# A gated delta-rule layer with a feed-forward block on one core: weights kept on chip for the eight items of a head, values turned on VectorE by way of DRAM, keys scaled on GpSimd, and all stages and transfers in a new order

## The reference

```python
qkvz = hidden_states @ W_qkvz          # per key head: q 128, k 128, v 2 x 128, z 2 x 128
mixed = silu(conv4(concat(q, k, v)))   # causal convolution over 4 tokens
beta, g = sigmoid(b), -exp(A_log) * softplus(a + dt_bias)
q, k = l2norm(q) * DK ** -0.5, l2norm(k)     # each key head serves two value heads
# by chunks of 64 tokens (the kernel takes chunks of 128):
T = inverse(I + tril(k_beta @ k.T * decay, -1))
v_new, k_cumdecay = T @ v_beta, T @ (k_beta * exp(g))
# step over the chunks of a sequence:
vn = v_i - k_cumdecay_i @ state
out = (q_i * exp(g_i)) @ state + (q_i @ k_i.T * decay_i) @ vn
state = state * exp(g_last) + (k_i * exp(g_last - g_i)).T @ vn
x = rmsnorm(core * silu(z)) * norm_weight
y = x.reshape(B, S, VD) @ W_out
```

## Time and profile before

| what | value |
|---|---|
| median of 3 runs | 4410.59 us (4410.58 to 4412.84) |
| time of the profiled execution | 4409.74 us |
| its span, first to last instruction | 4408.0 us |
| TensorE busy, weight loads | 4208.9 us (95%), 3698.7 us (84%) |
| ScalarE busy | 3843.0 us (87%) |
| VectorE busy | 3727.2 us (85%) |
| GpSimd busy | 2342.4 us (53%) |
| moved by DMA | 584.82 MB, mean 133 GB/s |

### The profile page before, as it was taken

How to read it: one execution, slowest core, us unless ns; L and a number is a source line. 1 busy time by engine, 2 the same in 40 slices (tenths; PEclk the granted TensorE clock), 3 DMA queues, 4 the chain that set the end, 5 groups by cost and what they waited for, 6 DMA issues and landing times. The chain is left out here.

```text
span 4408.0 us, 140088 instructions
## 1 busy us (share of the span) xinstructions
PE 4208.9 (95%) x44246; PEld 3698.7 (84%) x44246; DVE 3727.2 (85%) x6642; ACT 3843.0 (87%) x10855; POOL 2342.4 (53%) x3319
## 2 busy tenths in 40 slices
PE   3799999999999999999999999999999999999888
PEld 2688888888888888888888888888888888888745
DVE  5688888888888888888888888888888888888766
ACT  2699999999999999999999999999999999999755
POOL 3355555555555555555555555555555555555455
PEclk9999999999999999999999999999999999999999
DMA  5544444444444444444444434344444343434201
GB/s 182 180 131 146 130 145 133 142 134 141 134 140 135 140 135 140 139 136 139 136 142 132 145 130 146 129 143 132 147 128 150 125 153 122 153 123 154 72 6 34
DMA packets 450786, 584.82 MB, mean 133 GB/s; under 512 B 237472, under 2 KB 315552, under 8 KB 433184
## 3 DMA queue, kind: packets, MB, share of 16 engines
q1 hardware_dynamic: 449568, 575.59, 40.6%
q10 hardware_dynamic: 1152, 8.39, 0.5%
HBM read 533.81 MB, written 50.07 MB: 132 GB/s over the span
## 5 line engine op out<-in xcount | busy, mean ns | idle before, releaser
L1014 DVE SCALAR_TENSOR_TENSOR conv<-ps,cws,conv 128x511 f32<-128x511 f32 (+2 forms) x1536 | 1085.6, 742 | 59.8 <-ACT conv L892 39.9
L698 PE MATMUL ps<-xb,wb 128*128 128x512 f32 x3072 | 842.9, 409 | 25.7 <-DMA wb<-w_scratch 21.6
L698 PEld LDWEIGHTS ps<-xb,wb 128*128 128x128 f32 x3072 | 542.0, 190 | 127.5 <-issue 27.8
L1057 DVE CAST_PREDICATED pl<-masks,ps 128x512 f16<-128x512 uint16 x768 | 546.9, 712 | 55.3 <-PE ps L760 32.7
L953 ACT ACTIVATE t<-ps 128x512 f16<-128x512 f32 x768 | 465.9, 607 | 118.3 <-PE ps L768 107.1
L1263 POOL TENSOR_TENSOR xo<-xo,zs 128x512 f32<-128x512 f32 x128 | 163.8, 1280 | 717.0 <-DVE xo L1108 717.0
L1263 POOL TENSOR_TENSOR xo<-xo,home 128x512 f32<-128x512 f32 x128 | 162.8, 1272 | 699.4 <-DVE xo L1108 699.4
L957 ACT ACTIVATE u<-ps 128x512 f16<-128x512 f32 x768 | 473.2, 616 | 43.6 <-PE ps L773 43.6
L858 PE MATMUL ps<-wo,xt 128*128 128x256 f32 x3072 | 427.4, 289 | 33.6 <-DVE xt L1114 32.8
L712 PE MATMUL ps<-wb,xb 128*128 128x256 f32 x3072 | 428.5, 289 | 0.0
L858 PEld LDWEIGHTS ps<-wo,xt 128*128 128x128 f32 x3072 | 382.9, 190 | 47.7 <-issue 42.0
(11 more groups left out here) (188 smaller groups left out, 11701.8 us busy)
## 6 DMA issues: line engine op xcount, KB each, us to landing
xb<-x_scratch SPq DMA_DIRECT2D x128, 1024.0 KB, 5.9
wb<-w_scratch SPq DMA_DIRECT2D x128, 1024.0 KB, 5.6
decays<-rows_scratch SPq DMA_DIRECT2D x128, 512.0 KB, 3.7
wb<-w_scratch SPq DMA_DIRECT2D x128, 512.0 KB, 4.3
wo<-wout_scratch SPq DMA_DIRECT2D x128, 512.0 KB, 6.3
rk<-rk_scratch SPq DMA_DIRECT2D x128, 256.0 KB, 4.2
w_scratch<-wsplit SPq DMA_DIRECT2D x128, 192.0 KB, 3.2
wpiece<-in_Wqkvz SPq DMA_DIRECT2D x128, 96.0 KB, 2.5
```

The source lines that it names most:

```text
L698: last = nc.tensor.matmul(proj_bank[c][:, :], wb[:, pw, k * WCOL + c * D:k * WCOL + (c + 1) * D], xb[p][:, px, k * S:(k + 1) * S], start=( ...
L1014: nc.vector.scalar_tensor_tensor(out=conv[c][:, back:S], in0=proj_bank[c][:, 0:S - back], scalar=cws[p][:, c * TAPS + 3 - back:c * TAPS + ...
L1057: nc.vector.copy_predicated(halves(pl[l], l, 0), mask[:, None, :, :].broadcast_to([128, NU, C // (4 << l), 2 << l]), packed(p_bank, l)).th ...
```

## The change

1. Weights are loaded once per head: `load_w`, `load_wz` and `load_wout` do nothing for seven items of eight. `wo` is one buffer instead of two. SP runs a loop of eight steps (`steps_by_head`) for it.
2. The values are no longer turned on TensorE. `flip_v` on VectorE transposes 32x32 blocks of each `conv[V0]`, `conv[V1]` into `flip` (the memory of `et`), `store_v` writes the 512 KB to DRAM, and `load_v` reads them back in four transfers so that each token's channels come together in `vt[p]`, now laid out by 32-channel pieces. `values` on ScalarE is gone. `decay` now waits until the previous item's `store_v` has landed, since both use `et`.
3. `keys` runs on GpSimd.
4. `ORDER` is new in all its parts, offsets now from -3 to 2 (before from -2 to 3); PSUM banks are dealt anew, and the waits that guard them with it. `load_x` now stands at offset +1 in the first part of a step.

```diff
-        wo = [sb(f"wo{p}", [128, 2, R, H], f32r) for p in range(2)]
+        wo = sb("wo", [128, 2, R, H], f32r)
-        vt = [home[:, 1, :].rearrange("p (n h d) -> p n h d", n=NC, h=R), sb("vt1", [128, NC, R, D])]
+        vt = [home[:, 1, :].rearrange("p (w x) -> p w x", w=4), sb("vt1", [128, 4, R * NC * 32])]
+        flip = et[:, :, :].rearrange("p (q u) c -> p q (u c)", q=4)
-        proj_bank = (ps[5], ps[6], ps[5], ps[6])
-        z_bank = (ps[5], ps[6])
+        proj_bank = (ps[6], ps[7], ps[5], ps[7])
+        z_bank = (ps[6], ps[6])
-        turn_bank = (ps[7], ps[5], ps[7], ps[5])
-        gram_bank = (ps[6], ps[7])
-        o_turn_bank = (ps[7], ps[7])
-        out_bank = (ps[7], ps[7])
+        turn_bank = (ps[6], ps[7], None, None)
+        gram_bank = (ps[6], ps[5])
+        o_turn_bank = (ps[7], ps[5])
+        out_bank = (ps[5], ps[7])
...
-            + at(0, ("fix_mm", g1), ("ff_total", 0), ("fix", g0)) + at(1, ("project_z", g1)) + at(2, ("load_wz", 0)) + at(3, ("load_x", 0))
+            + at(-1, ("load_v", 0), ("ff_load", 2), ("ff_load", 0), ("fix_mm", g0), ("residual", 0)) + at(1, ("load_x", 0)) + at(-2, ("gate", g1))
...
-            def load_w(a, p, _):
+            def load_w(a, q, _):
+                if q:
+                    return
+                ws_out.wait(sp, a + B - 1 - LEAD, 32)
                 proj_mm.wait(sp, a - 1, 4)
-                rk_in.wait(sp, a - 1, 16)
...
+            def store_v(a, p, _):
+
+                sp.wait_ge(flipped.sem, flipped.at(a, 2))
+                vt_in.wait(sp, a - 1, 64)
+                sp.dma_start(v_dram[:, :, :], flip).then_inc(v_out.sem, 16)
+
+            def load_v(a, q, _):
+                p = q % 2
+                sp.wait_ge(v_out.sem, v_out.at(a, 16))
+                res_ready.wait(sp, a - 2, NC)
+                for w in range(4):
+                    sp.dma_start(vt[p][:, w, :], v_dram[w * 32:(w + 1) * 32].rearrange("r q x -> q r x")).then_inc(vt_in.sem, 16)
...
-            def values(a, p, h):
-                act.wait_ge(turn_mm.sem, turn_mm.at(a, h + 3))
-                res_ready.wait(act, a - 2, NC)
-                nc.scalar.activation(vt[p][:, :, h, :], four(turn_bank[V0 + h]), ACT.Copy).then_inc(vt_ready.sem, 1)
-
             def decay(a, p, g):
                 act.wait_ge(row_masked.sem, row_masked.at(a, g + 1))
                 act.wait_ge(cw_ready.sem, cw_ready.at(a, 1))
                 attn_ready.wait(act, a - 1, g + 1)
+                v_out.wait(act, a - 1, 16)
...
-            def keys(a, p, _):
-                ve.wait_ge(rk_in.sem, rk_in.at(a, 16))
+            def flip_v(a, p, h):
+
+                ve.wait_ge(silued.sem, silued.at(a, h + 3))
+                attn_ready.wait(ve, a, 2)
+                nc.vector.transpose(flip.rearrange("p q (h n c) -> p h q n c", h=R, n=NC)[:, h],
+                                    conv[V0 + h][:, :].rearrange("p (n q c) -> p q n c", n=NC, q=4)).then_inc(flipped.sem, 1)
...
                 if n == 0:
-                    ve.wait_ge(vt_ready.sem, vt_ready.at(b, 2))
+                    ve.wait_ge(vt_in.sem, vt_in.at(b, 64))
...
+            def keys(a, p, _):
+                pool.wait_ge(rk_in.sem, rk_in.at(a, 16))
+                pool.wait_ge(silued.sem, silued.at(a, 1))
+                ks_mm.wait(pool, a - 2, 3)
+                nc.gpsimd.tensor_tensor(kq[p][:, :, 0, :], conv[K][:, :].rearrange("p (n c) -> p n c", n=NC),
+                                        rk[:, :].rearrange("p (c n) -> p n c", n=NC), ALU.mult).then_inc(kq_ready.sem, 1)
```

More of the change, by code:

```diff
@@ L573, in delta_rule @@
-            + at(1, ("conv", V1, 3)) + at(0, ("u_copy", 5)) + at(1, ("mask_row", g1), ("keys", 0)) + at(0, ("t_copy", 5), ("ff_abs", 0),
-               ("ff_abs", 1)) + at(-1, ("intra_mm", 3)) + at(0, ("resid_mm", g0)) + at(1, ("turn", Q)) + at(-1, ("added", g0), ("out", 3),
-               ("ff_below", 2), ("ff_tern", 2)) + at(0, ("ff_set", 0), ("resid_mm", g1)) + at(1, ("gram", g0)) + at(-1, ("gate", g1))
-            + at(1, ("gram", g1)) + at(0, ("resid", g0)) + at(1, ("decay", g0), ("squares", Q), ("decay", g1)) + at(2, ("load_rows", 0))
@@ L581, in delta_rule @@
-            + at(2, ("project", K)) + at(0, ("y_copy", 0)) + at(1, ("u_first", g0)) + at(0, ("update_mm", 0), ("intra_mm", 0))
+            at(-1, ("t_mm", 5), ("u_mm", 5), ("z", g1)) + at(0, ("conv", V0, 3)) + at(-1, ("rnorm", Q)) + at(-2, ("o_rnorm", g0))
+            + at(-1, ("t_copy", 5), ("ff_abs", 0), ("ff_abs", 1), ("u_copy", 5)) + at(-3, ("out_mm", g0)) + at(-1, ("resid_mm", g0))
+            + at(0, ("conv", V1, 3)) + at(-1, ("resid_mm", g1)) + at(-2, ("intra_mm", 3)) + at(0, ("turn", Q), ("decay", g0), ("gram", g0))
@@ new lines, in delta_rule @@
+            + at(1, ("load_w", 0)) + at(-3, ("added", g0)) + at(0, ("squares", Q)) + at(-2, ("o_norm", g0)) + at(-1, ("resid", g0), ("resid", g1))
+            + at(-2, ("out", 3), ("ff_below", 2), ("ff_tern", 2)) + at(-1, ("ff_set", 0)) + at(0, ("gram", g1), ("system", g0), ("attn", g0))
+            + at(-1, ("load_v", 0), ("ff_load", 2), ("ff_load", 0), ("fix_mm", g0), ("residual", 0)) + at(1, ("load_x", 0)) + at(-2, ("gate", g1))
+            + at(0, ("decay", g1), ("system", g1)) + at(-1, ("fix_mm", g1), ("ff_total", 0)) + at(0, ("diagonal", g0)) + at(-1, ("fix", g0))
@@ L582, in delta_rule @@
+            + at(-1, ("out", 2)) + at(0, ("t_mm", 4)) + at(-1, ("residual", 3), ("ff_tern", 1), ("o_square", g0)) + at(0, ("t_copy", 4), ("u_mm", 4))
+            + at(1, ("conv", V0, 2)) + at(-1, ("qs_mm", 3), ("y", 3)) + at(0, ("p_mm", 5), ("z", g0), ("u_copy", 4)) + at(-1, ("q_part", 3))
+            + at(0, ("store_v", 0)) + at(1, ("conv", V1, 2), ("load_norm", 0), ("silu", Q)) + at(0, ("p", 5)) + at(-1, ("y_copy", 3))
+            + at(1, ("keys", 0)) + at(0, ("project_z", g1))
         )
@@ L598, in steps, with steps_by_head, step @@
                 step(s, s % 2)
+        def steps_by_head(engine, **parts):
+            def step(s, q):
+                for offset, stage, *n in ORDER:
+                    if stage in parts and not (isinstance(s, int) and not 0 <= s + offset < ITS):
+                        parts[stage](s + offset, (q + offset) % B, *n)
+            first, last = -(-(3 - NEAR) // B), (ITS - FAR) // B
+            for s in range(-FAR, first * B):
+                step(s, s % B)
+            with engine.Fori(first, last) as j:
+                for q in range(B):
+                    step(B * j + q, q)
+            for s in range(last * B, ITS - NEAR):
+                step(s, s % B)
         @block.sync
@@ L1179, in ff_ternary @@
                     link(nc.vector.tensor_tensor(m["fs"][:, 1:2], fscale[:, 0:1], fsud[:, :], ALU.mult))
[L1180 removed]
+            steps(ve, ff_set=ff_set, ff_halves=ff_halves, ff_below=ff_below, ff_tern=ff_ternary, conv=convolve, flip=flip_v, system=system, attn=attention, u_first=first, t_first_copy=t_first_copy, p=factor,
                   resid=resid, fix=fix, residual=residual, state=state, out=output, x_low=x_low, added=add)
```

136 lines of the change are left out of this document (69 added, 67 removed).

## The result

The changed kernel takes 4835.99 us (median of 4 runs, 4823.1 to 4841.23) against 4411.72 us (4410.58 to 4413.55) for the one before: ratio 1.0957, interval 1.0944 to 1.097. It is 424 us slower, and 524 us over the forecast. The profiled execution took 4823.1 us.

What follows compares the result with a forecast made beforehand. TensorE's own list of work was taken to set the period (30.99 of 31.42 us per step). Sum: 4410.6 - 116 (turns) + 10 (head starts) + 8 (start) = 4312 us; 8-in-10 range 4240 to 4450, forecast's own 4255 to 4385.

Steps and rivals of the forecast that it cites:

- The input, `load_x`: Input load between `project_z` g1 and the keys' projection: 7.45 us of room, 5.9 to 6.1 needed; cost 0.
- The late rival: Input or values land late on SP's queue; TensorE waits 1.5 us per step for `xb`: 4504 us, chance 0.20.
- Turns off TensorE, 0.91 us per item: Removing the two turns of values shortens TensorE's list by 0.91 us per item: 116 us less.
- packs tighter: Rival: TensorE's idle time goes to zero (floor 30.08 us per step), head starts cost nothing: 4247 us, chance 0.09.
- The order, "I let it stand": New `ORDER`: TensorE's 0.43 us of idle time per step may grow or go; left unchanged in the sum.
- VectorE as the bound: Rival: flips of 2.1 us each make VectorE set a period of 32.2 us: 4530 us, chance 0.06.
- Keys on GpSimd at 1.15: `keys` on GpSimd takes 1.15 us (between 1.04 and 1.28), hidden before `gram` with 2 to 3 us left.
- Values by DRAM: Store and reload of values take 9.3 us after the second flip; `residual` 0 waits 0 to 1.4 us; cost 0.
- Weights once per head, 0: Dropping 7/8 of 2 MB of weights per item gains 0, since no steady-stretch step waited for them.
- Head starts, 10 us more: At a head's first item, `wb` delays `load_v` and `load_x`; about 0.6 us reaches TensorE at 16 heads: 10 us more.
- `u_first`: No-change rival: `u_first` in its long form holds TensorE's `t_first`, giving back 0.82 us per step: 4417 us, chance 0.07.
- Start, 8 us: At program start, `yacc` loads of 8.59 us stand ahead of the third item's input: 8 us more.

Runs made afterwards that it cites:

- experiment 9: Changed kernel with the four `load_v` transfers cut by 32 tokens instead of 32 channels, so each begins with a dimension of 32: 4333.31 us, ratio 0.9824.
- experiment 5: Changed kernel with four `load_v` transfers in 1 KB pieces, the 128 rows first (values land in wrong places): 4288.53 us, ratio 0.9715.
- (3): Changed kernel with `load_v` as one plain 512 KB transfer, rearrangement left out (values land in wrong places): 4227.17 us, ratio 0.9582.
- experiment 6: Changed kernel with the rearrangement moved into the store (four transfers of 32 partitions) and one plain `load_v`; complete layer: 4240.04 us, ratio 0.9608.
- experiment 4: Changed kernel with eight extra 128x512 matmuls on TensorE just ahead of its wait for the input `xb`: 4685.65 us, ratio 1.0621.
- experiment 11: Kernel before, in its old order, with only the values' way exchanged for flips, the rearranging store and one plain load: 4471.39 us, ratio 1.0124.
- experiment 8: Kernel before with only `keys` moved to GpSimd, at its old place in the order: 4464.97 us, ratio 1.0114.
- experiment 1: Changed kernel with the input loaded for the first two items only, so later items use the wrong sequence: 4326.92 us, ratio 0.9808.
- experiment 2: Changed kernel with `load_x` issued ahead of `load_v` in SP's order: 5172.08 us, ratio 1.1724.
- experiment 7: Kernel before with only `wb` loaded once per head (both transfers), order as before: 4424.86 us, ratio 1.0024.
- experiment 10: Experiment 6 with `wb` loaded for each item again (both transfers), `wo` still once per head: 4291.68 us, ratio 0.9718.

## Why the prediction was wrong

**The step that failed** is in "*The input, `load_x`*": "The transfer needs 5.9, or 6.1 with the wake. If SP is free, 1.3 us remain." The room was as worked out (7.2 us from issue to need). The 5.9 us were not: they came from transfers with no narrow one just ahead, and the values' load keeps a quarter of the DMA engines busy for 6 us. The step of 2011.25 of the changed kernel shows it, with the four `load_v` issued from 1999.59 and the input at 2002.11:

```profile
2001.50:2004.00 2.50, 2.50 (x37) 2.32 (x36) 0.90 (x3) 2.35 (x5) 2.29 (x4) 1.00 0.27 95
2004.50:2007.00 2.50, 2.50 (x20) 2.32 (x18) 2.12 (x5) 2.49 (x14) 1.84 (x3) 1.00 1.07 315
2008.00:2009.00 1.00, 1.00 (x10) 1.00 (x10) 0.33 (x2) 1.00 (x8) 0.16 (x1) 1.00 0.27 109
```

Counted by size in the same trace, the packets in flight at a time are at first about four of 1 KB (values), then twelve of 8 KB (input) beside the four, and from 2008 to 2010 four of 8 KB: the last quarter of the input stood in line behind the values. In experiment 9 sixteen of 8 KB are in flight at once. The input took 9.2 us, and the experiments tie this to the first dimension of the values' load: with all rows first it is 6.6 (experiment 5), by 32 rows 6.4 (9), plain 5.6 (3). The prediction counted `load_v` as four issues of SP and 3.5 us to land, never as a load on engines that another transfer needs.

The Trainium skill (DMA: Bandwidth & Descriptors, "Why a DMA increments its semaphore by 16 and not by 1") has the rule that the prediction lacked: the number of DMA engines of a transfer is the largest one up to 16 that divides the slowest dimension on both sides. For the source `q r x` with a 4 in front, and 128 rows in the target, that is 4 of 16; the share of 0.25 to 0.27 and the four packets in flight agree, and so does the 0.75 with 32 in front. The page adds that such a transfer takes the lowest-numbered engines, by which all four parts would share the same four; the share fits, but no run here shows which engines they were.

**What the wait cost** had two parts, one of which the prediction did not have at all. TensorE's idle time is 3.0 us per step, 2.57 more than forecast. The slower clock behind it makes its list 31.53 us long, 1.45 more than the forecast floor and 1.69 more than the 29.84 of the same list in experiment 6; experiment 4 gives back at least 1.2 of it.

**The late rival** ("the input or the values come late", 0.20) had the place and the sign, and 4504 us. Its reason was wrong: it had the store taking 6.3 us, and the store took the 3.7 of the forecast. Its size was half of the wait (1.5 of 3.0 us) and nothing for the clock. That it named the right place is luck as far as its reason goes.

**The rest of the sum**, judged by experiment 6, where the input is in time:

- *Turns off TensorE, 0.91 us per item*, counted in full: "packs tighter", with 4247 us and a chance of 0.09, is what experiment 6 came to (4240.04), partly by luck. Its floor of 30.08 us was too high; TensorE is busy for 29.84 of 29.89 us, 24 us less in 128 steps than 30.08, and the rest of the program takes 17 us more than that case had. Where the 0.24 us come from was not tried.
- *The order, "I let it stand"*: this was a term, not a rest. The turns taken out of the old order cost 56 us (experiment 11), in the new order all of the kernel gains 174.
- *Flips at 0.7 us*: 0.70. *VectorE as the bound*: no.
- *Keys on GpSimd at 1.15*: 1.55, over the bound of 1.28. Hidden in the new order, not in the old (experiment 8, 51 us).
- *Values by DRAM*: `residual` 0 waits 1.9 us where 0 to 1.4 was given; no row of TensorE hangs on it while the input comes last. In experiment 1, with the input out of the way, `residual` 0 still waits 90 us in 43 steps and TensorE ahead of `y` 67 us in 30; that kernel is 87 us above experiment 6. Experiment 2 shows what a still later return costs.
- *Weights once per head, 0*: 11 us more in the old order (experiment 7), but 52 us less in the new one (experiment 10, `wb` alone). "None of it was waited for" read the old order's rows; in the new one the weights would compete for the input's slot.
- *Head starts, 10 us more*: in the changed kernel 28 waits are 3.2 us longer than the others, about 90 us, before the clock. In experiment 9 all waits after the start are 66 us, in experiment 6 they are 5 us (11 waits). The 11 us of experiment 7 are in another order and no measure of this term.
- *`u_first`* as the end of the gain: nothing; TensorE's idle time in experiment 6 is 3.3 of 2032.6 us.
- *Start, 8 us*: too small. In experiment 6 the third item's projection waits 13.80 us for its input, in the changed kernel 17.59; the kernel before has no such wait.

**Open**: how much of the 174 us is the new order alone, since no run has the new order with the turns left on TensorE. Which engines a narrow transfer takes, and what a first dimension between 4 and 32 does, was not tried either. Nor is it known why experiment 11's state copy comes late, whether from the flips' place or from their length.

## What to carry to other kernels

A transfer has a width as well as a size: read the share of the DMA engines while it runs, and give its rows, not a small factor, the first dimension. Before a landing time is taken from a row of before, ask what is issued in the microseconds ahead of it and on how many engines, and where TensorE will wait for as long as here (2 us), count also the slower clock behind it. And where a change moves work and writes a new order, try the parts apart: here each of the three parts tried was worth nothing or less in the old order, and all together 174 us once the values' transfers were wide.
